# Lag attention by even and odd output parts, with row statistics on ScalarE

## The reference

```python
def _autocorrelation(Q, K, V):            # Q = layernorm(x), K = V = ctx
    B, L, D = Q.shape
    ...
    qf = jnp.fft.fft(q, axis=2)
    kf = jnp.fft.fft(k, axis=2)
    corr = jnp.fft.ifft(qf * jnp.conj(kf), axis=2).real
    topk = int(C * np.log(L))
    w, idx = jax.lax.top_k(corr.transpose(0, 1, 3, 2), topk)
    w = jax.nn.softmax(w, axis=-1)
    pos = jnp.arange(L)[:, None]
    out = jnp.zeros_like(v)
    for i in range(topk):
        g = jnp.minimum(idx[:, :, None, :, i] + pos, L - 1)
        out = out + w[:, :, None, :, i] * jnp.take_along_axis(v, g, axis=2)
    return out.transpose(0, 2, 1, 3).reshape(B, L, D)
...
x = x + jnp.tanh(g_xattn[0]) * _L0_xattn_ref(_layernorm(x, axis=-1), ctx_4096, ctx_4096)
```

## Time and profile before

| | |
|---|---|
| time, median of 3 runs | 1353.75 us (1353.68 to 1356.89) |
| the profiled execution, its own time | 1356.5 us |
| span of the profiled execution | 1354.8 us |
| PE busy | 1239.7 us (92%) |
| DVE busy | 783.7 us (58%) |
| ACT busy | 513.5 us (38%) |
| POOL busy | 573.0 us (42%) |

### The profile page before, as it was taken

One profiled execution on the slowest core, in us unless ns is written; L12 is line 12 of the kernel. 1 busy time (PEld: TensorE's weight loads), 2 busy tenths in 40 slices (PEclk: granted clock), 3 DMA queues, 4 the chain that ended last, 5 costly groups with the idle time before them and its releaser, 6 DMA issues. The chain is left out here.

```text
span 1354.8 us, 20940 instructions
## 1 busy us (share of the span) xinstructions
PE 1239.7 (92%) x6442; PEld 846.7 (62%) x6442; DVE 783.7 (58%) x2026; ACT 513.5 (38%) x939; POOL 573.0 (42%) x931
## 2 busy tenths in 40 slices
PE   4799999999878999999999998999999999968886
PEld 2354544445435954458888786988888898635443
DVE  3889999998963680015433333444554443369885
ACT  2555545454423400023322222232222322168894
POOL 5667877777642001013221222523212231068884
PEclk8999999999988899999999999999999999879998
DMA  5211212302004502227778874535333331131111
GB/s 197 92 64 32 93 62 96 138 31 109 0 1 149 224 1 84 70 85 246 265 240 283 273 233 161 187 94 128 114 103 124 96 101 54 62 70 47 62 62 78
DMA packets 52481, 156.25 MB, mean 115 GB/s; under 512 B 5952, under 2 KB 16192, under 8 KB 52288
## 3 DMA queue, kind: packets, MB, share of 16 engines
q1 hardware_dynamic: 39152, 113.46, 23.6%
q0 software_dynamic: 13264, 41.95, 10.8%
HBM read 112.93 MB, written 45.61 MB: 117 GB/s over the span
## 5 line engine op out<-in xcount | busy, mean ns | idle before, releaser
L1210 PEld LDWEIGHTS ex_bank<-ex_xT,ex_gu 128*112 128x112 f32 x1248 | 140.4, 177 | 24.3 <-issue 23.3
L1210 PE MATMUL ex_bank<-ex_xT,ex_gu 128*112 128x128 f32 x1248 | 143.6, 273 | 2.0 <-issue 1.0
L44 PE MATMUL xa_bank<-fT_high,M_hi 128*128 128x256 f32 x512 | 144.0, 281 | 0.0
L46 PE MATMUL xa_bank<-fT_high,M_lo 128*128 128x256 f32 x512 | 143.0, 279 | 0.0
L45 PE MATMUL xa_bank<-fT_low,M_hi 128*128 128x256 f32 x512 | 142.9, 279 | 0.0
L52 PE MATMUL la_bank<-la_osum,la_tab 128*128 128x512 f32 x256 | 120.8, 617 | 24.1 <-POOL la_osum L291 23.7
L291 POOL TENSOR_TENSOR la_osum<-la_oprod 128x512 f32<-128x512 f32 x64 | 80.1, 1273 | 73.7 <-DVE la_oprod L479 73.7
L1074 POOL TENSOR_TENSOR ex_small<-listed,ex_small 128x1 int32<-128x1 int32 x42 | 15.4, 368 | 223.7 <-DVE Wk L1152 223.5
L52 PEld LDWEIGHTS la_bank<-la_osum,la_tab 128*128 128x128 f32 x256 | 47.7, 196 | 86.4 <-issue 48.6
L44 PEld LDWEIGHTS xa_bank<-fT_high,M_hi 128*128 128x128 f32 x512 | 96.7, 189 | 0.3
L46 PEld LDWEIGHTS xa_bank<-fT_high,M_lo 128*128 128x128 f32 x512 | 96.7, 189 | 0.0
(11 more groups left out here) (284 smaller groups left out, 2853.4 us busy)
## 6 DMA issues: line engine op xcount, KB each, us to landing
produced<-Wk SPq DMA_DIRECT2D x39, 512.0 KB
ex_gu<-in_gate_up SPq DMA_DIRECT2D x16, 896.0 KB
X<-in_x SPq DMA_DIRECT2D x8, 1024.0 KB, 7.4
la_v_raw<-in_ctx SPq DMA_DIRECT2D x16, 512.0 KB, 4.0
produced<-la_zeros SPq DMA_DIRECT2D x16, 512.0 KB, 4.7
normal<-rt_xn SPq DMA_DIRECT2D x16, 512.0 KB, 5.4
fT<-in_ctx_T SPq DMA_DIRECT2D x8, 1024.0 KB, 5.7
xa_f<-in_ctx SPq DMA_DIRECT2D x8, 1024.0 KB, 4.8
```

The source lines that it names most:

```text
L44: pe.matmul(out, a[0], b[0], start=first, stop=False)
L46: return pe.matmul(out, a[1], b[0], start=False, stop=last)
L1210: m = pe.matmul(bank[half][0:INTER, 0:P], gu[:, slot, at:at + INTER], xT[:, k, :], start=(k == 0), stop=(k == KD - 1))
```

## The change

The output is split another way. Around the middle, the kinds of the spectra are even or odd in the position: kinds 0 and 3 give a part that both halves share, kinds 1 and 2 one that they have with opposite signs. The even part (two matmuls, bank 0) is added to both row tiles, the odd part (two matmuls, bank 1) is added to one and subtracted from the other. The folds of the weights move to whole lags, which needs a copy of one column per group in `w_halves` and two more matmuls in `weight_spectra`. On DVE the products of the even part come first, then `c_products`, then the products of the odd part; POOL's sums follow in the same order. On PE the correlation moves ahead of the even part's rows. The statistics leave DVE but for the first three batches and the last: the odd part's adds also sum their results, and ACT takes the sums (first layer norm) and the squares with 128x1024 activations at three places in each step (`statistic`). The units of batch 1 are now written out ahead of the loop, which starts at batch 2.

```diff
+        KINDS = (0, 3, 1, 2)
+        part_bank = [bank[0], bank[1]]
...
             def w_halves(u, g):
...
-                a, b = wt[:, two, 0:P], wt[:, two, P:L]
-                pool.tensor_tensor(w_less[:, two, :], a, b, ALU.subtract).then_inc(s["w_fold"], 1)
+                a, b = wt[:, two, 1:P], wt[:, two, P + 1:L]
+                pool.tensor_tensor(w_less[:, two, 1:P], a, b, ALU.subtract).then_inc(s["w_fold"], 1)
+                pool.tensor_copy(w_less[:, two, 0:1], wt[:, two, P:P + 1]).then_inc(s["w_fold"], 1)
                 pool.tensor_tensor(a, a, b, ALU.add).then_inc(s["w_fold"], 1)
...
                 if before:
-                    for i in range(4):
-                        o_sum(before[0], i)
+                    o_sum(before[0], 0)
+                    o_sum(before[0], 1)
                 if after:
                     c_sums(after[0])
+                if before:
+                    o_sum(before[0], 2)
+                    o_sum(before[0], 3)
...
+                def squares(scales, b, j):
+                    act.activation(junk[:], rows(b, j), ACT.Square, bias=scales.less_mean[:, j:j + 1],
+                                   accum_out=scales.squares[:, j:j + 1]).then_inc(s["stat"], 1)
+
+                def sum_of(b, j):
+                    act.activation(junk[:], rows(b, j), ACT.Identity, accum_out=norm.sums[:, 0, 0, j:j + 1]).then_inc(s["stat"], 1)
...
                 if after:
                     spectra(after[0], True)
+                statistic(before2, now, 2)
                 if now:
                     share(now[0], 2)
                     exponent(now[0], 3)
...
                 def products():
                     if before:
-                        o_products(before[0], before[2])
+                        o_products(before[0], 0)
                     if after:
                         c_products(after[0], after[2])
+                    if before:
+                        o_products(before[0], 1)
...
-                if before2 and before2[2] == 1 and not (isinstance(before2[1], int) and before2[1] == B - 1):
-                    at_least(dve, s["added0"], before2[0] + 1)
-                    at_least(dve, s["added1"], before2[0] + 1)
-                    scales_after.variance(dve, X, before2[1])
-                if due is not None:
+                if due is not None and fixed(due) and due <= 2:
                     dve.wait_ge(x_in, 16 * (due + 1))
                     norm.variance(dve, X, due)
...
                 at_least(pe, s["wt_ready"], 2 * u + 2)
                 full_product(pe, bank[6][:], lags_t(2), more)
                 full_product(pe, bank[7][:], lags_t(3), less)
-                at_least(pe, s["added0"], u)
-                full_product(pe, bank[4][:], lags_t(0), more)
-                full_product(pe, bank[5][:], lags_t(1), less).then_inc(s["wspec"], 1)
+                full_product(pe, bank[4][:], lags_t(0), more, True, False)
+                full_product(pe, bank[4][:], last_t(2), less, False, True)
+                full_product(pe, bank[5][:], lags_t(1), less, True, False)
+                full_product(pe, bank[5][:], sign_t, more, False, True).then_inc(s["wspec"], 1)
...
                 if after:
                     spectra(*after)
-                if before:
-                    positions(before[0], 0)
                 if after:
...
                     correlate(after[0])
+                if before:
+                    positions(before[0], 0)
```

More of the change, by code:

```diff
@@ L163, in lag_t, with pos_t @@
             return table(LAG_AT + kind * L, L)
-        def pos_t(kind, j):
-            return table(POS_AT + (2 * kind + j) * P, P)
+        def pos_t(kind):
+            return table(POS_AT + kind * P, P)
+        sign_t = table(SIGN_AT, P)
         names = """gw_in tab_in tab_rest gate_in Wq_in zeroed filled consts dchain
@@ L196, in one @@
                 step(on, due)
-            for u in range(-2, 2):
+            for u in range(-2, 4):
                 one(u, u // 2, u % 2)
-            with eng.Fori(1, B - 2) as b:
+            with eng.Fori(2, B - 2) as b:
                 one(2 * b, b, 0)
@@ L324, in _ @@
             act.wait_ge(s["consts"], 2)
+            act.wait_ge(s["tgd"], 1)
+            act.activation(less_tg[:], tg[:], ACT.Copy, scale=-1.0).then_inc(s["less_gate"], 1)
             def normalise(u, b, h, j):
@@ L378, in step @@
             def step(on, due):
-                now, after, next2 = on(0), on(1), on(2)
+                before2, now, after, next2 = on(-2), on(0), on(1), on(2)
                 if now:
                     exponent(now[0], 0)
+                statistic(before2, now, 0)
+                if now:
                     exponent(now[0], 1)
+                statistic(before2, now, 1)
+                if now:
                     share(now[0], 0)
@@ L475, in o_products @@
                 pairs = (((0, 4), (2, 5)), ((2, 4), (1, 5)), ((3, 6), (4, 7)), ((4, 6), (3, 7)))
-                for i, two in enumerate(pairs):
+                for i in (2 * part, 2 * part + 1):
+                    two = pairs[KINDS[i]]
                     at_least(dve, s["osums"], 4 * u + (i - 1 if i >= 2 else 0))
@@ L628, in __init__ @@
         self.mv = sb("mv", [P, 2, 2])
-        small = sb("small", [P, 12, 2])
-        self.var, self.root, self.power, self.eps, self.step, self.spare, self.less, self.half, self.more, self.now, self.other, self.one = (small[:, i, :] for i in range(12))
+        small = sb("small", [P, 16, 2])
+        (self.var, self.root, self.power, self.eps, self.step, self.spare, self.less, self.half, self.more, self.now, self.other, self.one,
+         self.part, self.less_part, self.less_mean, self.squares) = (small[:, i, :] for i in range(16))
+        self.sums = sb("sums", [P, 2, 2, 2])
         self.scale, self.shift = (sb(n, [P, TILES]) for n in ("scale", "shift"))
     def signal_with(self, sem):
-        self.chain, self.var_ready, self.set, self.links, self.taken, self.ready = (
-            sem(f"{self.tag}_{n}") for n in ("chain", "var_ready", "set", "links", "taken", "ready"))
+        self.chain, self.var_ready, self.set, self.links, self.taken, self.ready, self.summed, self.mean_ready = (
+            sem(f"{self.tag}_{n}") for n in ("chain", "var_ready", "set", "links", "taken", "ready", "summed", "mean_ready"))
     def prepare(self, pool):
-        for column, value in ((self.power, -0.5), (self.eps, EPS), (self.less, -1.0), (self.half, -0.5), (self.more, 1.5), (self.one, 1.0)):
+        for column, value in ((self.power, -0.5), (self.eps, EPS), (self.less, -1.0), (self.half, -0.5), (self.more, 1.5), (self.one, 1.0),
+                              (self.part, 1.0 / D), (self.less_part, -1.0 / D)):
             pool.memset(column, value).then_inc(self.set, 1)
@@ L663, in on_pool, with means_on_pool, on_pool_from_squares, link @@
         pool.wait_ge(self.ready, n + 1)
+    def means_on_pool(self, pool, b):
+        now = self.sums[:, bass.ds(b % 2, 1), :, :].rearrange("p o h j -> p (o h) j")
+        pool.tensor_tensor(self.var, now[:, 0, :], now[:, 1, :], ALU.add).then_inc(self.summed, 1)
+        pool.wait_ge(self.summed, b + 1)
+        pool.tensor_tensor(self.less_mean, self.var, self.less_part, ALU.mult).then_inc(self.mean_ready, 1)
+    def on_pool_from_squares(self, pool, b):
+        def link(i, out, one, two, op):
+            pool.tensor_tensor(out, one, two, op).then_inc(self.links, 1)
+            pool.wait_ge(self.links, self.STEPS * b + i)
+        link(1, self.var, self.squares, self.part, ALU.mult)
+        link(2, self.var, self.var, self.eps, ALU.add)
+        link(3, self.root, self.var, self.power, ALU.pow)
+        link(4, self.step, self.root, self.root, ALU.mult)
+        link(5, self.step, self.step, self.var, ALU.mult)
+        link(6, self.step, self.step, self.half, ALU.mult)
+        link(7, self.step, self.step, self.more, ALU.add)
+        link(8, self.now, self.root, self.step, ALU.mult)
+        pool.tensor_tensor(self.scale[:, bass.ds(2 * b, 2)], self.now, self.one, ALU.mult)
+        pool.tensor_tensor(self.shift[:, bass.ds(2 * b, 2)], self.less_mean, self.now, ALU.mult).then_inc(self.ready, 1)
+        pool.wait_ge(self.ready, b + 1)
     def variance(self, dve, X, b, n=None):
```

141 lines of the change are left out of this document (95 added, 46 removed).

## The result

The changed kernel took 1357.68 us (median of 20 runs, 1352.52 to 1361.45), the kernel before 1353.6 (20 runs, 1349.52 to 1356.89). The ratio is 1.0032, 95% interval [1.002, 1.0044]: slower by 0.32%, some 4 us. That lies inside the forecast range and on the wrong side of the forecast, which was 3 us faster.

What follows compares the result with a forecast made beforehand. Lag attention was taken as bound by a race of loops through four engines, at 23.4 against 23.62 us per unit. 13 units gave -2.8, start +1.1, end -1.6: -3.3, so 1350.5 us from median 1353.75, range 1343 to 1359.

Steps and rivals of the forecast that it cites:

- one by the exponent: Lag attention's loop from output products through transposes, exponent and masking of column 0: 22.85, or 23.45 us with the q fold.
- the named places: DVE idles 0.1 to 0.7 us ahead of the spectra products, and again ahead of even adds and column 0's masking.
- Rival C: Lag attention's loops are shorter than reckoned and DVE's own work decides: 21.8 us per unit, 1330 in all; chance 0.08.
- D: ACT's third pass, from about 1.8 us, delays column 3's exponent and masking: loops 24.2, whole 1361; chance 0.16 shared.
- The bound set for "wrong": Distance between spectra products under 22.8 or over 24 us, or ACT's passes over 1.8, would refute the forecast.
- Loop 1: Lag attention's loop from PE's spectra through DVE's products, column 3, POOL's fold and transposes to next spectra: 23.46 us.
- I take one of each: 23.4.: Column 3's masking beats POOL's second fold in one unit (loops 23.1), loses in another (23.7): 23.4 us; chance 0.32.
- S to the spectra products: 5.28.: From the start of PE's spectra to DVE's spectra products, read from the v spectra's release: 5.28 us.
- forecast +1.1: Start of the stage: unit 2's spectra products come up to 2.6 us earlier, but 2.39 of odd products follow: +1.1.
- the forecast of -1.6: End of the stage: adds end 2.3 us earlier in the mean, less 0.7 for longer weight spectra: -1.6.
- "same" and "slower": Whole kernel's time: slower means above 1357.8 us, chance 0.19; faster below 1349.7, 0.43; same is the rest, 0.38.
- B: Column 3's masking always loses to POOL's second fold: loops 23.7 us, whole 1354.3; chance 0.20.

Runs made afterwards that it cites:

- the early fold: Changed kernel with POOL folding the first two columns' weights at the head of its step, not behind the four sums: 1352.69 us, ratio 0.9987 to the kernel before.
- the second pair of profiles: Both kernels profiled again unedited: changed kernel 1361.06 us (6 runs, ratio 1.0066), kernel before 1350.51 us (one run).
- with PE kept busy: Unused matmuls in PE's gaps at the stage's end: 17 in the changed kernel, 1353.52 us (ratio 0.9994); 14 in the kernel before, 1352.09 us (0.999).
- the kernel with old orders and new split: Changed kernel with the earlier orders on DVE, POOL and PE, even/odd parts and ACT statistics kept: 1355.28 us, ratio 1.001 to the kernel before.
- the best time, 1345.30: Changed kernel with the early fold and 17 unused matmuls in PE's gaps at the stage's end: 1345.30 us, ratio 0.9933 to the kernel before.
- the version with the v spectra first: Changed kernel with the next unit's even v spectra ahead of the weight spectra on PE: 1359.14 us, ratio 1.0056 to the kernel before.
- the version with one more matmul in the gap: Changed kernel with the early fold, early even v spectra, end matmuls and last odd v matmul written twice: 1348.67 us, ratio 0.996 to the kernel before.

## Why the prediction was wrong

**Right in the main mechanism.** Two loops of nearly equal length bound the step, one by PE's spectra and one by the exponent; the freed DVE time turned into idle time at the named places; no clean gain came from DVE's busy time. Two terms of the sum were mis-sized, and the average hid a third thing. Rival C (21.8 per unit) fell for the reason given, and D by ACT's 0.98 of spare time. The bound set for "wrong", a distance over 24, was just reached: 23.99 and 24.05 in turn. Loop 1's terms against the rows after, in the step shown:

| term | forecast | measured |
|---|---|---|
| PE's spectra to spectra products | 5.28 | 205.79 - 200.21 = 5.58 |
| spectra and odd products | 4.78 | 210.59 - 205.79 = 4.80 |
| rest of column 3 | 3.41 | 214.10 - 210.59 = 3.51 |
| reciprocal to transposes | 2.25 | 216.38 - 214.10 = 2.28 |
| transposes to next spectra | 7.74 | 224.18 - 216.38 = 7.80 |
| sum | 23.46 | 23.97 |

**First step that failed: "I take one of each: 23.4."** Column 3's masking does not win in half of the steps. It lost in 13 of 14: 0.90 in the step read, 0.97 in the next (236.99). POOL starts the operation 212.88 - 205.79 = 7.09 after the spectra products, the masking comes at 7.21. The prediction had 7.15 to 7.25 against 7.20. The rival in which it always loses (23.7) was the right branch, and the early fold's -0.5 per unit proves the price.

**Second: "S to the spectra products: 5.28."** That term was read from PE's own wake (226.53), the only engine that waited there before. PE again starts 5.28 after S (205.49), but DVE starts only at 205.79. In the loop DVE starts 0.36 us after the end of ACT's copy (204.86 + 0.57 = 205.43). The 23.7 of the right branch and this 0.30 are the measured 24.0, though not term by term: the branch priced the hold at 0.6 and it was 0.47 (0.55 in every other step), and the remaining terms ran 0.1 over. Leaving the slack in the path of a different waiter was the error: the row named the moment at which PE, and not DVE, could go on.

**The step that was not read: which units the average holds.** The distances of before, all 13 from the same timeline as the earlier trace rows, are not alike. Take first the eight whose code is looped in both kernels (units 4 to 11). Before, they alternate between 24.1 and 22.97, 23.54 in the mean. The alternation is column 0's masking: it meets POOL's fold of q and takes 1.4 to 1.5 us in every other step and 0.43 in the rest, the two values of the earlier trace rows. In the other five units before takes 23.76. After, the eight take 24.01 and the five 23.48. So the change loses 0.47 in eight units, +3.75 us, and gains 0.28 in five, -1.39: +2.36.

After, those five are all written out. In the kernel before, whose loop begins one batch earlier, only the last three are (23.83, 23.82 and 23.87), and the first two are looped (24.08 and 23.21). So 0.36 of the 1.39 gained comes in units that the change also took out of the loop, and how much of it is the split's is not shown. In the written-out steps the forecast of 23.4 is nearly met, because the second error is absent there: from PE's spectra (320.24) to the spectra products (325.40) it is 5.16. The masking is held there too (0.83 in that step). The idle time ahead of the odd adds is absent there as well (0.04 in place of 0.60 and 0.30).

**The ends.** Start: forecast +1.1 (bounds -0.2 and +2.4), measured 62.87 - 63.54 = -0.67, below its lower bound, and -1.02 in the second pair of profiles: the forecast had charged 2.39 for odd products there, but the first of them run at 65.27, behind unit 2's spectra products, and none stand ahead of them. From unit 15's products to the last add: 51.87 before, 51.45 after, -0.4 against the forecast of -1.6, inside its bounds of -3 and +4; in the second pair it is 53.07 against 51.16, +1.9, with PE's rows and weight spectra from 396 us on slower than in the first (the last rows 5.61 in place of 5.28). The clock has a large part in it: with PE kept busy this stretch takes 49.59 in the changed kernel. But it takes 48.09 in the kernel before with PE kept busy, so with the clock up in both the new end is 1.5 us longer, not shorter. Sum measured: -0.67 + 2.36 - 0.42 = +1.3 in this pair of profiles, +2.4 in the mean of two pairs, against -3.3.

**What stays open.** The stage accounts for 2.4 of the 4.1 us between the medians. The half clock at the entry to routing is worth 3 us when it falls, and two profiles of each kernel cannot say how often it does; the experts' section scatters between profiles from 314.5 to 318.3 us. Nor was it tried why the looped steps of the kernel with old orders and new split are 0.36 longer than before's (23.90 against 23.54); POOL's added copy of 0.18 to 0.20, the masking of 0.90 against 0.78 in the earlier trace rows, and DVE's idle time ahead of the odd adds, 0.45 in the mean against 0.29, are candidates. The early fold was not tried in the kernel before, where the masking of column 3 is held too (0.78), nor was the move of the statistics alone; so it is not shown that the new split has any part in the best time, 1345.30.

**Chances.** The result lies at the edge between "same" and "slower". B was given 0.20 and priced at 1354.3; with the 0.30 it gives 13 x 0.3 = 3.9 more, 1358.2, and the measured median is 1357.7. That agreement is luck in part, since five of the units did not pay it.

## What to carry to other kernels

When a loop of waits bounds the step, busy time taken from an engine turns into waiting; look instead for the collision inside the chain, here two elementwise engines on one memory for 0.5 us per unit, which moving one fold earlier took off the path. Where an order leaves an edge on the path that another engine waited on before, its price is that of the new waiter. Before trusting an average distance, list all distances: looped and written-out steps of the same code differ. And look at what the tensor engine does before the last dependent chain: 17 unused matmuls in its gaps were worth 4 us in the changed order and 7 in the one with the early fold, though 14 such matmuls gained the kernel before only some 1.6, not clear of noise.

## What the runs showed of the hardware

- DVE's start after ACT's copy: 0.36 us in the looped steps (205.43 to 205.79), 0.09 in the written-out ones (348.78 to 348.87); PE's start after the same copy: 0.06 and 0.05. The trace shows a part of the 0.36: in the looped step DVE's queue runs a semaphore instruction (0.02), ALU_OP (0.05) and FUSED_REGOPS (0.12) between 205.4 and 205.8; in the written-out step it has no register instruction there. The view of this line over the whole run has 24 of them, three for each of the eight looped units:

```profile
L504 DVEq FUSED_REGOPS  x24: 57/57/123, 133.5 to 302.0; - x24
```

- Ahead of the odd adds it is the same: three FUSED_REGOPS of 0.05 to 0.15 in the gap of 0.60, one of 0.06 in that of 0.30, none in that of 0.04. That these instructions fill the gaps is read from their times; no run took them out.
- The tensor engine's clock with the same 2.1 to 2.4 us of idle time ahead of each correlation fell in alternate steps of the loop and in 9 of 14 in all (5.41 and 3.72), and stayed up in all but the last of the correlations of the version with the v spectra first (idle 2.30, another 1.23 ahead of the transposes). So the length of that gap alone doesn't decide; in the version with one more matmul in the gap (1.35 to 1.47 idle) all correlations took 3.7.
- A third pass over 1024 columns with a sum costs ACT 1.04 to 1.15 and a separate read of 0.20; an accumulating add costs DVE a read of 0.08 that lies under the next operation, so a step of 0.67 to 0.68, as without it.
- The hold is shorter than what was left of POOL's operation, by some 0.15 in the three cases read: 0.47 of 0.61 (213.00), 0.35 of 0.50 and 1.02 of 1.18. It works both ways: POOL's copy of two elements took 0.38 instead of 0.19 when DVE's masking (0.61) met it.
